# MLP: the 64-row products of fc1 in pairs, six tiles of a pass held open together

## The chip, the cores and the metric

One core of a Trainium2 chip (trn2) runs the whole program. The metric is the device time of one execution in microseconds (us), as the median of several runs. Engines are named as in the profile: PE is TensorE (PEld its weight loads), DVE is VectorE, ACT is ScalarE, POOL is GpSimd, SP is the engine that issues the DMAs.

## The reference

One transformer block with modulation on x of 2 x 2048 tokens by 576 channels. Only its last part matters here:

```
C = 576; FF = 2304
h = modulate(layernorm(x), shift_mlp, scale_mlp)
mlp = gelu(h @ W_fc1 + b_fc1, approximate=True) @ W_fc2 + b_fc2
x = x + gate_mlp * mlp
```

The contraction of fc1 has 576 terms: four blocks of 128 and a last one of 64.

## The kernel before

The program runs in phases, one after the other; attention takes the largest part, and `phase_mlp` is the last. Tokens go in 8 chunks of 512 (`CH`, `NCH = 8`), hidden channels in two halves of 1152 (`FF // 2`). A pass n (0 to 15, `NN`) takes one chunk through one half: passes 0 to 7 the first half, 8 to 15 the second; `ORDER` sets which chunk.

**fc1 of a pass** makes 9 tiles (`NT`; f = 0 to 8) of 128 hidden channels by 512 tokens, each in one PSUM bank. Every float32 operand is split into a high and a low part of type fp32r. For each of the four blocks of 128 rows there are three products (high x high, high x low of the tokens, low of the weights x high). The last block has 64 rows only. `wm` holds its high weights twice, in rows 0 to 63 and again in 64 to 127; `hh[..][:, 4, :]` holds the tokens' high part in rows 0 to 63 and their low part in 64 to 127, so that one product gives both terms. `wr` holds the low weights in rows 0 to 63 and zeros in 64 to 127 (a memset on POOL, awaited through `s_z`); product 14 of a tile multiplies it by the same 128 rows. So a tile is 14 products of 128 rows (`passes`, L42 on), a pass 126.

**fc2 of a pass** makes 8 tiles (4 groups of 128 tokens by 2 halves of 288 channels), each from 27 products (9 f by 3), in the four banks `pm`. fc1 uses the four banks `pf` in turn (pass 0 also `pm`).

The order on each engine is written out by hand, and semaphores tie them. Per f: PE ends tile f and raises `s_f1`; ACT applies gelu (L2110) into `af[m % 2]`, after the low part of tile f-2 is done (`s_al`); DVE writes the high part `ah` (CAST, L2060) and the low part `al` (TENSOR_TENSOR, L2062). The first tile of fc2 waits for `s_al` of f ahead of its products with f. Two further jobs are hung on the same f loop of ACT and DVE:

- in passes whose successor's tokens are still whole in DRAM (n + 1 in `WHOLE`, that is n = 1 to 6 and 9 to 14), ACT splits one block of the next pass's tokens after the gelu of f = 2 to 6 (`high_h`, L2099), DVE makes its low part (`low_h`, L2045 and L2048);
- in pass 8, after each f one piece of W_fc2's second half: `high` on ACT (L2090), `low` on DVE (L2038). fc2 of pass 8 waits for piece f too ahead of its first products with f.

DVE ends each fc2 tile with two operations (L2075, L2081). POOL adds a bias to a block of y (L2129) once it has landed. PE's sequence in a pass is 126 products of fc1, then 216 of fc2.

Of the kernel before, what the change touches and what calls it, by code (L numbers as in the profile page):

```python
# [7 lines left out]
F = mybir.dt.float32  # L8
# [230 lines left out]
class Ahead:  # L239
# [4 lines left out]
    def __init__(self, S, hh, hl, b1, new, kf):  # L244
        self.hh, self.hl, self.b1 = hh, hl, b1
        self.oi = S.sb("oi", [128, KT, CH])
        stg = self.oi[:, :, :].rearrange("p k t -> p (k t)")
        self.stg = [stg[:, i * C:(i + 1) * C] for i in range(4)]
        self.pf = [S.ps(f"pf{i}", [128, 512]) for i in range(4)]
        G = FF // 6  # L250
        self.wide = [stg[:, i * G:(i + 1) * G] for i in range(6)] + [kf[:, i * G:(i + 1) * G] for i in range(4)]
        self.wh, self.wl, self.wm, self.wr = new
        self.s_w, self.s_f1, self.s_b1, self.s_hs = S.sems("w", 4), S.sem("f1"), S.sem("b1"), S.sem("hs")
        self.s_whi, self.s_wlo, self.s_z = S.sem("whi"), S.sem("wlo"), S.sem("z")

    def load(self, e, j, W):

# [8 lines left out]
    def split(self, j):  # L266

        g, kt = divmod(j, KT)
        cols = slice(g * FF // 6, (g + 1) * FF // 6)
        return (self.wh[:, kt, cols], self.wl[:, kt, cols]) if kt < 4 else (self.wm[:, cols], self.wr[0:64, cols])  # L270


class FirstThird:
# [26 lines left out]
    def low(self, e, kt, stg):  # L300
        w = stg[kt % 2]
        e.wait_ge(self.hi, kt + 1)
        if kt < 4:
            e.tensor_tensor(self.wl[:, kt, :], w[:, self.n], self.wh[:, kt, :].bitcast(F), ALU.subtract).then_inc(
                self.lo, 1)
        else:
            e.tensor_tensor(self.wr[0:64, :], w[0:64, self.n], self.wm[0:64, :].bitcast(F), ALU.subtract).then_inc(
                self.lo, 1)


def program(nc, x, cond, W_qkv, b_qkv, W_proj, b_proj, W_fc1, b_fc1, W_fc2, b_fc2, W_ada, b_ada, out):
# [1094 lines left out]
def phase_proj(nc, A, W, rest, first, N, ident, ks0, adaT, eps, gd, xf, ot, sm, W_fc1, b_fc1, hth, htl, hw,  # L1406
# [366 lines left out]
    def gpsimd(e):  # L1773
        rest.add(e)
        for kind, c, n in work():
# [26 lines left out]
            elif kind == "weights":  # L1802
                if n == 0:
# [5 lines left out]
                    e.wait_ge(N.s_z, 1)  # L1809
                hi, lo = N.split(n)  # L1810
                rows = slice(0, 128 if n < 4 else 64)
                e.wait_ge(N.s_whi, n + 1)
                e.tensor_tensor(lo, N.wide[n][rows], hi[rows].bitcast(F), ALU.subtract).then_inc(N.s_wlo, 1)

    with nc.Block() as block:
        block.sync(sync)
# [6 lines left out]
def phase_mlp(nc, A, first, N, gd, hth, htl, hw, y1, y2, of, W_fc1, b_fc1, W_fc2, b_fc2):  # L1823
# [38 lines left out]
    def piece(k):  # L1862

        half, j = divmod(k, 24)
        if j < 15:
            g, kt = divmod(j, 5)
            cs, c0 = slice((g - 1) * G3, g * G3), half * FH + g * G3
            if g == 0:
                to = (first.wh[:, kt, :], first.wl[:, kt, :]) if kt < 4 else (first.wm, first.wr[0:64, :])
            else:  # L1870
                to = (wh[:, kt, cs], wl[:, kt, cs]) if kt < 4 else (wm[:, cs], wr[0:64, cs])
            return (W_fc1, kt * 128, 128 if kt < 4 else 64, c0, G3) + to
        j -= 15
        return W_fc2, half * FH + j * 128, 128, 0, C, vh[:, j, :], vl[:, j, :]
# [46 lines left out]
    def sync(e):  # L1921
# [11 lines left out]
        def load(n):  # L1933
# [44 lines left out]
        for i in range(4):  # L1978
            e.wait_ge(s_w[i], total[i])
        for i in range(2):  # L1980
            e.wait_ge(s_h[i], 32)
            e.wait_ge(s_yi[i], 32 * NN)
            e.wait_ge(s_yo[i], 32 * NN)
        e.wait_ge(N.s_hs, 64)
# [1 line left out]
        e.wait_ge(s_c, 64)  # L1986

    def tensor(e):
        for n in range(NN):
            i, half = n % 2, n // NCH  # L1990
            if n in WHOLE:
                e.wait_ge(s_hlo, KT * WHOLE.index(n) + KT)
            elif n > 1:
                e.wait_ge(s_h[i], 32)
            for f in range(4 if n == 0 else 0, NT):
                m = NT * n + f
                if n in (0, NCH) and f % 3 == 0:
                    e.wait_ge(s_whi, W1[half] + 5 * (f // 3 + 1) - DONE)
                    e.wait_ge(s_wlo, W1[half] + 5 * (f // 3 + 1) - DONE)
                if m > 7:  # L2000
                    e.wait_ge(s_af, m - 3)
                if f < 3:
                    pairs = passes(first.wh, first.wl, first.wm, first.wr, hh[i], hl[i],
                                   slice(f * 128, f * 128 + 128), slice(0, CH))
                else:
                    pairs = passes(wh, wl, wm, wr, hh[i], hl[i], slice((f - 3) * 128, (f - 3) * 128 + 128),
                                   slice(0, CH))
                for p, (w, a) in enumerate(pairs):
                    ins = e.matmul(tile(m)[:, :], w, a, start=p == 0, stop=p == 13)  # L2009
                ins.then_inc(s_f1, 1)  # L2010
            for t in range(4):
                ts = slice(t * 128, t * 128 + 128)
                for n2 in range(2):
                    m = 8 * n + 2 * t + n2
                    cs = slice(n2 * HALF, (n2 + 1) * HALF)
                    if m > 3:
                        e.wait_ge(s_ug, m - 3)
                    else:
                        e.wait_ge(s_af, m + 5)
# [65 lines left out]
    def scalar(e):  # L2085
# [6 lines left out]
        def high_h(n, kt):  # L2092

            e.wait_ge(s_hw, 48 * (WHOLE.index(n) + 1))
            if kt == 0:
                e.wait_ge(s_f1, NT * (n - 1))
                if n == 3:
                    e.wait_ge(N.s_hs, 64)
            e.activation(hh[n % 2][:, kt, :], hw_in[:, kt, :], ACT.Copy).then_inc(s_hhi, 1)  # L2099

        for n in range(NN):
            half = n // NCH
            for f in range(NT):
# [53 lines left out]
```

## Time and profile before

| | us |
|---|---|
| median of 3 runs | 3420.9 (3420.76 to 3423.96) |
| profiled execution | 3421.19 |
| its span, first to last instruction | 3419.5 |
| PE busy | 3403.6 (100% of the span) |
| DVE busy | 1982.8 (58%) |
| ACT busy | 1488.7 (44%) |

The profiled execution stands 0.3 us over the median; 1.7 us of it lie outside the span. A row of the timeline begins with its start in us from the span's start and its duration in us; durations of neighbours on one engine overlap, since each holds the time through the pipeline, so the pace is read from starts.

### The profile page before, as it was taken

What the parts mean: (1) busy time and instruction counts of PE and PEld (TensorE: products, weight loads), DVE (VectorE), ACT (ScalarE), POOL (GpSimd) and SP (SyncE); (2) the same over time, 40 slices, a digit from 0 to 9 for tenths busy, and PEclk for the clock granted to TensorE, in tenths of its full rate; (3) what the DMA queues carried; (4) which work ended last, traced back from release to release, by engine and by line L of the source; (5) the groups of instructions that cost most, each with busy time, mean ns of one, the idle gap of its engine ahead of it and who ended that gap; (6) DMA issues with size and microseconds to landing.
All of it is one profiled execution on the core that took longest, in us unless ns stands there. A gap on an engine that the chain in (4) does not pass through costs nothing. (4 is left out here: it accounts for less than half of the span.)

```text
span 3419.5 us, 46642 instructions
## 1 busy us (share of the span) xinstructions
PE 3403.6 (100%) x17036; PEld 2281.4 (67%) x17036; DVE 1982.8 (58%) x3592; ACT 1488.7 (44%) x2793; POOL 361.6 (11%) x284
## 2 busy tenths in 40 slices
PE   9999999999999999999999999999999999999999
PEld 7888854544545545545545545447989999898988
DVE  6446576776776766776766766754653333433332
ACT  3322365555555555555555555565531111211110
POOL 0000010111100000010000000015610101000000
PEclk9999999999999999999999999999999999999999
DMA  7553421212112121111211111115751212321211
GB/s 229 177 185 108 155 78 30 65 41 61 38 34 51 31 55 30 47 40 33 55 31 51 34 36 49 31 39 163 262 165 51 80 51 95 121 83 44 77 53 53
DMA packets 131908, 265.89 MB, mean 78 GB/s; under 512 B 17427, under 2 KB 38675, under 8 KB 124770
## 3 DMA queue, kind: packets, MB, share of 16 engines
q1 hardware_dynamic: 131686, 262.91, 25.5%
q8 instruction: 142, 2.33, 0.3%
q14 instruction: 80, 0.66, 0.1%
HBM read 164.50 MB, written 97.26 MB: 77 GB/s over the span
## 5 line engine op out<-in xcount | busy, mean ns | idle before, releaser
L1259 DVE TENSOR_REDUCE q_mx<-b_sp 128x1 f32<-128x512 f32 x1968 | 1196.3, 677 | 228.1 <-PE b_sp L1197 228.1
L1316 ACT ACTIVATE b_pt<-b_st 128x512 f32<-128x512 f32 x2009 | 1013.4, 626 | 441.2 <-PE b_st L1214 434.0
L1227 PE MATMUL b_op<-b_pt,b_vs 128*37 128x512 f32 x4096 | 929.4, 596 | 0.0
L1227 PEld LDWEIGHTS b_op<-b_pt,b_vs 128*37 128x37 f32 x4096 | 223.6, 113 | 567.3 <-issue 440.3
L2110 ACT ACTIVATE d_af<-n_pf,q_mx 128x512 f32<-128x512 f32 x140 | 96.3, 688 | 702.0 <-PE n_pf L2009 701.5
L2027 PE MATMUL d_pm<-d_vh,d_ah 128*128 128x288 f32 x1152 | 339.3, 295 | 0.5 <-DVE d_al L2062 0.5
L2028 PE MATMUL d_pm<-d_vl,d_ah 128*128 128x288 f32 x1152 | 339.4, 295 | 0.0
L2029 PE MATMUL d_pm<-d_vh,d_al 128*128 128x288 f32 x1152 | 339.3, 295 | 0.0
L1382 POOL TENSOR_TENSOR w_oc<-b_oa,b_ob 37x512 f32<-37x512 f32 x127 | 163.0, 1283 | 1588.4 <-DVE b_ob L1292 1582.3
L1197 PE MATMUL b_sp<-q_hh,q_lo 108*128 108x512 f32 x688 | 284.2, 413 | 0.9 <-PEq L1001 0.9
L1214 PE MATMUL b_st<-q_qs,q_ks 110*128 110x512 f32 x697 | 275.4, 396 | 0.0
L1214 PE MATMUL b_st<-q_lo,q_hh 110*128 110x512 f32 x672 | 264.0, 397 | 0.0
L1197 PE MATMUL b_sp<-q_ks,q_qs 108*128 108x512 f32 x640 | 263.7, 412 | 0.0
L1197 PE MATMUL b_sp<-b_ks,b_qs 108*128 108x512 f32 x640 | 263.6, 412 | 0.0
L1292 DVE COPY b_ob<-b_op 37x512 f32<-37x512 f32 x127 | 86.7, 683 | 292.3 <-PE b_op L1227 292.3
L1214 PE MATMUL b_st<-b_qs,b_ks 110*128 110x512 f32 x640 | 253.3, 396 | 0.0
L1324 ACT ACTIVATE b_oa<-b_op 37x512 f32<-37x512 f32 x127 | 75.6, 595 | 347.8 <-PE b_op L1227 347.8
L2027 PEld LDWEIGHTS d_pm<-d_vh,d_ah 128*128 128x128 f32 x1152 | 216.2, 188 | 1.4 <-issue 0.7
L2028 PEld LDWEIGHTS d_pm<-d_vl,d_ah 128*128 128x128 f32 x1152 | 216.1, 188 | 0.7
L2029 PEld LDWEIGHTS d_pm<-d_vh,d_al 128*128 128x128 f32 x1152 | 216.2, 188 | 0.0
L2075 DVE TENSOR_TENSOR d_ug<-d_pm,d_gt 128x288 f32<-128x288 f32 x128 | 58.5, 457 | 250.8 <-PE d_pm L2029 250.7
L2060 DVE CAST d_ah<-d_af 128x512 fp32r<-128x512 f32 x144 | 63.3, 440 | 240.9 <-ACT d_af L2110 240.9
(366 smaller groups left out, 4755.0 us busy)
## 6 DMA issues: line engine op xcount, KB each, us to landing
qkh<-a_th SPq DMA_DIRECT2D x72, 256.0 KB, 2.0
qkl<-a_tl SPq DMA_DIRECT2D x72, 256.0 KB, 2.1
d_yi<-y SPq DMA_DIRECT2D x64, 288.0 KB, 3.0
n_oi<-hw SPq DMA_DIRECT2D x12, 1024.0 KB, 5.9
vd<-a_vx SPq DMA_DIRECT2D x8, 1184.0 KB, 6.3
b_vs<-vd SPq DMA_DIRECT2D x32, 296.0 KB, 2.8
a_x<-in_x SPq DMA_DIRECT2D x8, 1152.0 KB, 6.3
ot<-w_oc SPq DMA_DIRECT2D x128, 72.0 KB
```

What stands on the lines that cost most here:

```text
L1197: e.matmul(sp[slot % 4][:, :], qs[i][0:108, qb * 128:qb * 128 + 128], ks[i][0:108, k4 * 512:k4 * 512 + 512], start=True, stop=True).then_i ...
L1214: e.matmul(bank(x)[:, :], ks[i][0:110, kb * 128:kb * 128 + 128], qs[i][0:110, u * 512:u * 512 + 512], start=True, stop=True).then_inc(s_st, 1)
L1227: ins = e.matmul(op[64 * a:64 * a + VW, :], vs[h % 2][:, 2 * j + a, :], pt[g % NP][:, a * 512:a * 512 + 512], start=j == 0, stop=j == 7)
L1259: e.tensor_reduce(mx[:, k // 4, k % 4:k % 4 + 1], sp[slot % 4][:, :], AX.X, ALU.max).then_inc(s_mx, 1)
L1292: e.tensor_copy(ob[i][:, :], op[0:VW, :]).then_inc(s_oa, 1)
L1316: e.activation(pt[g % NP][:, a * 512:a * 512 + 512], bank(x)[:, :], ACT.Exp, scale=SCALE).then_inc(s_p, 1)
L1324: e.activation(oa[i][:, :], op[64:64 + VW, :], ACT.Copy).then_inc(s_oa, 1)
L1382: e.tensor_tensor(oc[i][:, :], oa[i][:, :], ob[i][:, :], ALU.add).then_inc(s_oc, 1)
L2027: e.matmul(out, ah[:, f, ts], vh[:, f, cs], start=f == 0, stop=False)
L2028: e.matmul(out, ah[:, f, ts], vl[:, f, cs], start=False, stop=False)
L2029: ins = e.matmul(out, al[:, f, ts], vh[:, f, cs], start=False, stop=f == NT - 1)
L2110: e.activation(af[m % 2][:, :], tile(m)[:, :], ACT.Gelu_apprx_tanh, bias=b1[:, half * NT + f:half * NT + f + 1]).then_inc(s_af, 1)
```

## The change

fc1 uses a ring of eight banks (`pf` and `pm`). In passes 1 to 15 tiles 0 to 5 (`GROUP = 6`) run 13 products each and stay open. After tile 5's 13th the six last products follow in a row (`last_products`): those of even f use rows 0 to 63 of `wr` and `hh`, those of odd f rows 64 to 127 of `wr` and of a new tensor `hx`, a copy of the tokens' high part of the last block in rows 64 to 127. `wr` now holds the low weights in both halves; memset and `s_z` are gone. Tiles 6 to 8 have 14 products as before, and so has pass 0. `hx` lies in parts of old tensors and is written by an additional ACT copy ahead of the split of block 4, or by an additional DMA for passes 1, 8 and 9.

```diff
         g, kt = divmod(j, KT)
-        return (self.wh[:, kt, cols], self.wl[:, kt, cols]) if kt < 4 else (self.wm[:, cols], self.wr[0:64, cols])
+        return (self.wh[:, kt, cols], self.wl[:, kt, cols]) if kt < 4 else (self.wm[:, cols], self.wr[:, cols])
...
+        self.hx = [w[64:128, :, FF // 6:FF // 6 + 128] for w in (w0.wl, w0.wh)]
...
-                    e.memset(N.wr[64:128, :].bitcast(F), 0.0).then_inc(N.s_z, 1)
-                    e.wait_ge(N.s_z, 1)
...
-    def tile(m):
-        return pm[m - 4] if 4 <= m < 8 else pf[m % 4]
+    def bank(n, f):
+        ring = pf + pm if n == 0 else pf[0:1] + pm + pf[1:4]
+        return ring[f % 8]
+    GROUP = 6
...
+            e.dma_start(hx[i].bitcast(F), hth[4, 0:64, rows].rearrange("p (k t) -> p k t", k=4)).then_inc(s_h[i], 16)
+        e.dma_start(hx[1].bitcast(F), hh[1][0:64, 4, :].bitcast(F).rearrange("p (k t) -> p k t", k=4)).then_inc(s_h[1], 16)
...
+        def bank_free(n, f):
+            if f >= 8:
+                e.wait_ge(s_af, NT * n + f - 8 + 1)
+            elif n and 1 <= f < 5:
+                e.wait_ge(s_ug, 8 * (n - 1) + 4 + f)
+            elif n:
+                e.wait_ge(s_af, NT * n)
+        def last_products(n):
+            i = n % 2
+            if n == 1:
+                e.wait_ge(s_h[i], 16)
+            for f in range(GROUP):
+                w, c0 = (first.wr, f * 128) if f < 3 else (wr, (f - 3) * 128)
+                if f % 2 == 0:
+                    e.matmul(bank(n, f)[:, :], w[0:64, c0:c0 + 128], hh[i][0:64, 4, :], start=False,
+                             stop=True).then_inc(s_f1, 1)
+                else:
+                    e.matmul(bank(n, f)[:, :], w[64:128, c0:c0 + 128], hx[i], start=False, stop=True).then_inc(s_f1, 1)
...
-                if m > 7:
-                    e.wait_ge(s_af, m - 3)
+                bank_free(n, f)
...
-                for p, (w, a) in enumerate(pairs):
+                for p, (w, a) in enumerate(pairs[0:13] if grouped else pairs):
...
+                if grouped and f == GROUP - 1:
+                    last_products(n)
...
+            if kt == 4:
+                e.activation(hx[n % 2], hw_in[64:128, kt, :].rearrange("p (k t) -> p k t", k=4), ACT.Copy)
             e.activation(hh[n % 2][:, kt, :], hw_in[:, kt, :], ACT.Copy).then_inc(s_hhi, 1)
```

PE before, pass 2, where tile 0 ends and tile 1 begins (`q_hh0` is `hh[0]`, `e_wr0` the first third of `wr`):

```order
L2009 MATMUL n_pf2<-q_hh0,e_wl0 128x512
L2009 MATMUL n_pf2<-q_hh0,e_wm0 128x512
L2009 MATMUL n_pf2<-q_hh0,e_wr0 128x512
L2009 MATMUL n_pf3<-q_hh0,e_wh0 128x512 [waits d_s_af]
L2009 MATMUL n_pf3<-q_lo0,e_wh0 128x512
```

PE of the changed kernel, pass 2, where tile 5's 13th product ends and tile 6 begins (`e_wl0` stands for `hx[0]`, `z_wr` for the rest of `wr`):

```order
L2034 MATMUL n_pf1<-q_hh0,z_wl 128x512
L2034 MATMUL n_pf1<-q_hh0,z_wm 128x512
L2010 MATMUL n_pf0<-q_hh0,e_wr0 128x512
L2013 MATMUL d_pm0<-e_wl0,e_wr0 128x512
L2010 MATMUL d_pm1<-q_hh0,e_wr0 128x512
L2013 MATMUL d_pm2<-e_wl0,z_wr 128x512
L2010 MATMUL d_pm3<-q_hh0,z_wr 128x512
L2013 MATMUL n_pf1<-e_wl0,z_wr 128x512
L2034 MATMUL n_pf2<-q_hh0,z_wh 128x512 [waits d_s_af]
```

The last product of tile 0, which stood ahead of tile 1, now stands behind tile 5's 13th, and with it `s_f1` of tiles 0 to 4 comes later.

ACT before, around the split of block 4 for the next pass (`n_oi` holds the landed tokens):

```order
L2099 ACTIVATE q_hh0<-n_oi 128x512 [waits d_s_hw]
L2110 ACTIVATE d_af1<-n_pf3,q_mx 128x512 [waits d_s_al,n_s_f1]
L2099 ACTIVATE q_hh0<-n_oi 128x512 [waits d_s_hw]
L2110 ACTIVATE d_af0<-n_pf0,q_mx 128x512 [waits d_s_al,n_s_f1]
```

The same place of the changed kernel:

```order
L2129 ACTIVATE q_hh0<-n_oi 128x512 [waits d_s_hw]
L2140 ACTIVATE d_af1<-n_pf2,q_mx 128x512 [waits d_s_al,n_s_f1]
L2128 ACTIVATE e_wl0<-n_oi 64x4x128 [waits d_s_hw]
L2129 ACTIVATE q_hh0<-n_oi 128x512
L2140 ACTIVATE d_af0<-n_pf3,q_mx 128x512 [waits d_s_al,n_s_f1]
```

One copy is added; the order of the rest, and all of DVE's order in the f loop, is the same.

## Rows read from the trace of the kernel before

**Rows 1.** The page, part 1: busy time and share of each engine.

```profile
PE 3403.6 (100%) x17036; PEld 2281.4 (67%) x17036; DVE 1982.8 (58%) x3592; ACT 1488.7 (44%) x2793; POOL 361.6 (11%) x284
```

**Rows 2.** PE's waits, 2480 us to the end: waiter, releaser, us, times, longest.

```profile
PE d_pm L2027 <- DVE d_al L2062: 0.5, 1, 0.5
PE d_pm L2009 <- PEq L1815: 0.3, 1, 0.3
```

**Rows 3.** Timeline, PE: fc1 and fc2 of pass 4, first product of pass 5.

```profile
2721.60 0.40 PE L2009 MATMUL n_pf<-q_hh,e_wh 128*128 128x512 f32 x1
...
2750.60 0.40 PE L2009 MATMUL n_pf<-q_hh,z_wr 128*128 128x512 f32 x1
2750.84 0.30 PE L2027 MATMUL d_pm<-d_vh,d_ah 128*128 128x288 f32 x1
2750.97 0.30 PE L2028 MATMUL d_pm<-d_vl,d_ah 128*128 128x288 f32 x1
...
2779.48 0.39 PE L2009 MATMUL n_pf<-e_ah,e_wh 128*128 128x512 f32 x1
```

**Rows 4.** Timeline, PE, attention: out of and into products in column halves (L1227).

```profile
1499.78 1.89 PE L1227 MATMUL b_op<-b_pt,b_vs 128*37 128x512 f32 x8
1501.60 0.50 PE L1197 MATMUL b_sp<-q_hh,q_lo 108*128 108x512 f32 x1
1501.93 0.39 PE L1214 MATMUL b_st<-b_qs,b_ks 110*128 110x512 f32 x1
...
1505.24 0.39 PE L1214 MATMUL b_st<-b_qs,b_ks 110*128 110x512 f32 x1
1505.56 0.63 PE L1227 MATMUL b_op<-b_pt,b_vs 128*37 128x512 f32 x2
```

**Rows 5.** Timeline, PEld then PE, near 55 us: products of 64 rows (L668).

```profile
54.87 0.09 PEld L668 LDWEIGHTS a_sp<-a_wa,g_sc 128*2 128x2 f32 x2 [0.15 <-issue]
55.45 0.09 PEld L668 LDWEIGHTS a_sp<-a_wa,g_sc 64*2 64x2 f32 x4 [0.49 <-issue]
...
54.87 0.66 PE L668 MATMUL a_sp<-a_wa,g_sc 128*2 128x288 f32 x4
...
55.69 0.41 PE L668 MATMUL a_sp<-a_wa,g_sc 64*2 64x288 f32 x2
56.03 0.50 PE L705 MATMUL a_pm<-q_hh,a_wh 128*128 128x512 f32 x1
56.37 0.39 PE L705 MATMUL a_pm<-q_lo,a_wh 128*128 128x512 f32 x1
56.60 0.40 PE L705 MATMUL a_pm<-q_hh,a_wl 128*128 128x512 f32 x1
```

**Rows 6.** Timeline, DVE, pass 4: tiles 2 and 3, and tile 6.

```profile
2732.16 1.33 DVE L2060 CAST d_ah<-d_af 128x512 fp32r<-128x512 f32 x1 [2.05 <-ACT d_af L2110]
2733.53 0.69 DVE L2062 TENSOR_TENSOR d_al<-d_af,d_ah 128x512 fp32r<-128x512 f32 x1
2734.14 0.69 DVE L2045 TENSOR_TENSOR q_qs<-n_oi,e_ah 128x512 fp32r<-128x512 f32 x1
...
2745.69 0.69 DVE L2062 TENSOR_TENSOR d_al<-d_af,d_ah 128x512 fp32r<-128x512 f32 x1
2746.41 0.69 DVE L2048 TENSOR_TENSOR e_ah<-n_oi,e_ah 64x512 fp32r<-64x512 f32 x1
```

**Rows 7.** Timeline, DVE, pass 0, behind its work: no idle time between rows.

```profile
2512.45 0.42 DVE L2060 CAST d_ah<-d_af 128x512 fp32r<-128x512 f32 x1
2512.90 0.69 DVE L2062 TENSOR_TENSOR d_al<-d_af,d_ah 128x512 fp32r<-128x512 f32 x1
2513.51 0.42 DVE L2060 CAST d_ah<-d_af 128x512 fp32r<-128x512 f32 x1
```

**Rows 8.** Timeline, DVE, pass 8: two tiles in a row without idle time.

```profile
2968.64 0.42 DVE L2060 CAST d_ah<-d_af 128x512 fp32r<-128x512 f32 x1
2969.10 0.69 DVE L2062 TENSOR_TENSOR d_al<-d_af,d_ah 128x512 fp32r<-128x512 f32 x1
2969.71 0.75 DVE L2038 TENSOR_TENSOR d_vl<-n_oi,d_vh 128x576 fp32r<-128x576 f32 x1
2970.38 0.42 DVE L2060 CAST d_ah<-d_af 128x512 fp32r<-128x512 f32 x1
```

**Rows 9.** Timeline, ACT, pass 4: gelu and split.

```profile
2725.03 0.69 ACT L2110 ACTIVATE d_af<-n_pf,q_mx 128x512 f32<-128x512 f32 x1 [31.16 <-PE n_pf L2009]
...
2731.44 0.69 ACT L2110 ACTIVATE d_af<-n_pf,q_mx 128x512 f32<-128x512 f32 x1 [2.52 <-PE n_pf L2009]
2732.03 0.62 ACT L2099 ACTIVATE e_ah<-n_oi 128x512 fp32r<-128x512 f32 x1
```

**Rows 10.** Timeline, POOL: the memset ahead of `phase_mlp`, and pass 4.

```profile
2486.16 0.73 POOL L1808 MEMSET z_wr<- 64x768 f32 x1 [11.69 <-PE n_pf L1651]
...
2731.78 1.43 POOL L2129 TENSOR_TENSOR d_yi<-d_yi,d_gb 128x576 f32<-128x576 f32 x1 [11.39 <-DMA d_yi<-y]
```

**Rows 11.** DMA issues: KB each, median us from issue to landing.

```profile
n_oi<-in_L_cond_W_fc SPq DMA_DIRECT2D x18, 288.0 KB, 4.4
```

More of the change, by code:

```diff
@@ L253, in __init__ @@
         self.s_w, self.s_f1, self.s_b1, self.s_hs = S.sems("w", 4), S.sem("f1"), S.sem("b1"), S.sem("hs")
-        self.s_whi, self.s_wlo, self.s_z = S.sem("whi"), S.sem("wlo"), S.sem("z")
+        self.s_whi, self.s_wlo = S.sem("whi"), S.sem("wlo")
     def load(self, e, j, W):
@@ L306, in low @@
         else:
-            e.tensor_tensor(self.wr[0:64, :], w[0:64, self.n], self.wm[0:64, :].bitcast(F), ALU.subtract).then_inc(
-                self.lo, 1)
+            e.tensor_tensor(self.wr, w[:, self.n], self.wm.bitcast(F), ALU.subtract).then_inc(self.lo, 1)
 def program(nc, x, cond, W_qkv, b_qkv, W_proj, b_proj, W_fc1, b_fc1, W_fc2, b_fc2, W_ada, b_ada, out):
@@ L1807, in gpsimd @@
                     e.wait_ge(first.lo, KT)
-                    e.memset(N.wr[64:128, :].bitcast(F), 0.0).then_inc(N.s_z, 1)
-                    e.wait_ge(N.s_z, 1)
                 hi, lo = N.split(n)
-                rows = slice(0, 128 if n < 4 else 64)
                 e.wait_ge(N.s_whi, n + 1)
-                e.tensor_tensor(lo, N.wide[n][rows], hi[rows].bitcast(F), ALU.subtract).then_inc(N.s_wlo, 1)
+                e.tensor_tensor(lo, N.wide[n], hi.bitcast(F), ALU.subtract).then_inc(N.s_wlo, 1)
     with nc.Block() as block:
@@ L1838, in phase_mlp @@
     hh, hl = N.hh, N.hl
+    hx = first.hx
     af = [A.sb(f"af{i}", [128, CH]) for i in range(2)]
@@ L1868, in piece @@
             if g == 0:
-                to = (first.wh[:, kt, :], first.wl[:, kt, :]) if kt < 4 else (first.wm, first.wr[0:64, :])
+                to = (first.wh[:, kt, :], first.wl[:, kt, :]) if kt < 4 else (first.wm, first.wr)
             else:
-                to = (wh[:, kt, cs], wl[:, kt, cs]) if kt < 4 else (wm[:, cs], wr[0:64, cs])
+                to = (wh[:, kt, cs], wl[:, kt, cs]) if kt < 4 else (wm[:, cs], wr[:, cs])
             return (W_fc1, kt * 128, 128 if kt < 4 else 64, c0, G3) + to
@@ L1980, in sync @@
         for i in range(2):
-            e.wait_ge(s_h[i], 32)
+            e.wait_ge(s_h[i], (48, 64)[i])
             e.wait_ge(s_yi[i], 32 * NN)
@@ L1993, in tensor @@
             elif n > 1:
-                e.wait_ge(s_h[i], 32)
+                e.wait_ge(s_h[i], (48, 64)[i])
             for f in range(4 if n == 0 else 0, NT):
-                m = NT * n + f
+                grouped = n and f < GROUP
                 if n in (0, NCH) and f % 3 == 0:
@@ L2007, in tensor @@
                                    slice(0, CH))
-                for p, (w, a) in enumerate(pairs):
-                    ins = e.matmul(tile(m)[:, :], w, a, start=p == 0, stop=p == 13)
-                ins.then_inc(s_f1, 1)
+                for p, (w, a) in enumerate(pairs[0:13] if grouped else pairs):
+                    ins = e.matmul(bank(n, f)[:, :], w, a, start=p == 0, stop=p == 13)
+                if not grouped:
+                    ins.then_inc(s_f1, 1)
+                if grouped and f == GROUP - 1:
+                    last_products(n)
             for t in range(4):
@@ L2015, in tensor @@
                     cs = slice(n2 * HALF, (n2 + 1) * HALF)
-                    if m > 3:
+                    if m % 8 < 4:
+                        e.wait_ge(s_af, NT * n + m % 4 + (5 if n == 0 else 2))
+                    else:
                         e.wait_ge(s_ug, m - 3)
-                    else:
-                        e.wait_ge(s_af, m + 5)
                     for f in range(NT):
@@ L2033, in low @@
         def low(k):
-            src, _, rows, _, cols, hi, lo = piece(k)
+            cols, hi, lo = piece(k)[4:7]
             there(e, k)
@@ L2037, in low @@
             old_read(e, k)
-            e.tensor_tensor(lo, staged(k)[0:rows, 0:cols], hi[0:rows].bitcast(F), ALU.subtract).then_inc(s_wlo, 1)
+            e.tensor_tensor(lo, staged(k)[:, 0:cols], hi.bitcast(F), ALU.subtract).then_inc(s_wlo, 1)
         def low_h(n, kt):
@@ L2109, in scalar @@
                     e.wait_ge(s_al, m - 1)
-                e.activation(af[m % 2][:, :], tile(m)[:, :], ACT.Gelu_apprx_tanh,
+                e.activation(af[m % 2][:, :], bank(n, f)[:, :], ACT.Gelu_apprx_tanh,
                              bias=b1[:, half * NT + f:half * NT + f + 1]).then_inc(s_af, 1)
```

## The prediction

> **What bounds the kernel now.** First the page's busy times: PE is busy for 3403.6 of 3419.5 us, DVE for 58% and ACT for 44% [rows 1]. Then PE's waits in the last 940 us, which hold `phase_mlp`: two, of 0.5 and 0.3 us, both in pass 0 [rows 2]. So passes 1 to 15 are an unbroken stream of products, and only two things can change the time: how long PE's own stream is, and a wait that does not exist today. The granted clock is 1.00 throughout, the upper of its two levels (2.4 GHz), and I expect it to stay.
>
> Next the pace of that stream, from starts on PE's timeline [rows 3]. fc1 of pass 4 has 126 products; the first starts at 2721.60, the last at 2750.60: 29.00 / 125 = 0.232 us each. fc2 has 216 from 2750.84 to the next pass at 2779.48: 28.64 / 216 = 0.1326 each.
>
> **Part 1: PE's stream.** Removed per pass: six products of 128 rows, 6 x 0.232 = 1.39 us. Added: three pairs of 64 rows. Nothing in the trace shows two products side by side in the two halves of the rows. Nearest are the products in the two halves of the columns: eight of them take four steps, (1.89 - 0.59) / 3 = 0.43 us per pair, and one alone would need that much, since these are plain float32 products in two runs [rows 4]. So pairs do overlap there, and I take 0.232 us for a pair. Bounds: 0.43 / 2 = 0.215 below; 0.464 (no overlap at all) above.
>
> The array is then used in another division, and the trace has a price for going there and back. Out of the column halves: the last pair starts at 1499.78 + 1.89 - 0.59 = 1501.08, the next product at 1501.60, that is 0.52 for a pair of 0.43, so 0.09 more; the product after that starts 0.33 later and not 0.23, so 0.10 more, and its neighbour's record is 0.50 long for 0.39: its weight load is not hidden [rows 4]. Into them: 1505.24 to 1505.56 is 0.32 for 0.23, again 0.09 more [rows 4]; the weights there have 37 columns only, here 128, so I take the 0.10 for the load too. Does it also hold for rows? Going from 128 to 64 rows near 55 us, a pair that starts near 55.12 is followed at 55.45, and that one by the next at 55.69: 0.33 against 0.24; going back, 55.69 to 56.03 to 56.37 is 0.34 and 0.34 against 0.24 and 0.23 [rows 5]. The same 0.09 to 0.10 and 0.10. So the group costs 3 x 0.232 + 2 x (0.09 + 0.10) + 0.01 for the second product of a pair = 1.09 us (1.087), and a pass gains 1.39 - 1.09 = 0.30 us. Fifteen passes: **4.5 us gained**, of 10.4 that halving the six products alone would give.
>
> Two rules of the Trainium skill would make this less. TensorE: Matmul & The Clock Gate (Part 3, Measured speedup) reports 3.07 times for four row tiles, not 4; as an estimate from that share a pair would take 0.30 us, and the gain fall by 3.2 us in all. The same page (Part 3, the per-tile semaphore tail) puts 26 ns on each further increment of a semaphore in a group; six products here raise `s_f1`, an estimated 2 us over 15 passes if PE had to wait for them. No run so far shows either; the sum leaves both out.
>
> **Part 2: what waits for the group.** `s_f1` of tiles 0 to 5 now comes almost at once, some 18 us into fc1, and ACT and DVE have tiles 6 to 8 and the start of fc2 to do what they did during the whole of fc1. ACT's steps are shorter than DVE's (gelu to split starts 0.59 apart [rows 9]; the added copy for `hx`, some 0.6, stands once between tiles 6 and 7), and gelu of f needs only `al` of f-2, so DVE sets the pace. Its costs without idle time: CAST to TENSOR_TENSOR 0.45, on to the next CAST 0.61, a tile 1.06 [rows 7]; with a split of 512 columns another 0.61, a tile 1.68 [rows 6, 7]; tile 6 with the split of the half block 0.72 in place of 0.61 [rows 6], 1.79.
>
> Let E be the start of the first pair. Tile 0 ends at E + 0.50, gelu starts 0.02 later (in pass 4 tile 0 ends near 2725.01, gelu starts at 2725.03 [rows 3, 9]), and the CAST 0.72 after gelu's start (2731.44 to 2732.16 [rows 6, 9]): E + 1.24. The CAST of tile 8 starts 1.06 x 2 + 1.68 x 4 + 1.79 + 1.06 = 11.69 later, and `al` of 8 is ready after 0.45 + 0.69 + 0.03 more: **E + 14.10**. PE needs it at: the pairs and the way back, E + 0.89; tiles 6 to 8, 0.10 + 42 x 0.232 = 9.84, so fc2 starts at E + 10.73; 24 products later, 3.18, it wants f = 8: **E + 13.91**. So PE waits 0.19 us, in the 12 passes with splits: **2.3 us lost**. In passes 7 and 15 DVE has nothing else and keeps up with PE: tile 8 ends 0.16 into fc2, `al` is ready 0.02 + 0.72 + 0.45 + 0.69 + 0.03 later, at 2.07, 1.1 ahead of the 3.18. In pass 1 to 6 today one CAST takes 1.33 instead of 0.43 while POOL works [rows 6, 10]; that falls 10 us into the pass, where DVE now has no tile, so it costs nothing.
>
> In **pass 8** each tile has a piece of W_fc2: 2968.64 to 2970.38, 1.74 a tile [rows 8]. Piece 8 is ready at E + 1.24 + 8 x 1.74 + 0.46 + 0.61 + 0.75 + 0.03 = E + 17.01, wanted at E + 13.91: **3.1 us lost**. Piece f+4 is requested when piece f is done, lands 4.4 us later [rows 11], and is used 4 x 1.74 = 7 after the request, its ACT copy of 0.7 included: about 1 us to spare.
>
> **Part 3: the rest.** The wider low parts run over more partitions at the same columns, so at the same time; the memset on POOL ended near 2486.9 [rows 10] and PE never waited for it [rows 2]. The additional DMAs for `hx` stand in SP's queue ahead of the weight pieces of passes 0 and 8, half a microsecond each: in pass 8 the pieces are wanted 18 us later than now, so it is hidden; in pass 0 the first pieces are wanted early, where PE already waits 0.5 us [rows 2], at most 0.5 more. Banks: tile 8 waits for gelu of tile 0, started 6 us before; tiles 1 to 4 wait for the last fc2 tiles of the pass before, at least one tile of 3 us ahead. Nothing to pay.
>
> **Sum.** 3421.19 - 4.5 + 2.3 + 3.1 = 3422.1 for the profiled execution, which is 0.3 above the median of its kernel: **3421.8 us**, 0.9 over today's median. About 0.2% (6.8 us) is what a measurement of this kernel can tell from no change.
>
> **Rivals.**
> - *No overlap of the pairs.* Six products in a row at 0.232 plus the two changes of division: 6 x 0.232 + 0.38 = 1.77 for 1.39, +0.38 a pass, +5.7 us; DVE then has 0.7 us more per pass, so the 2.3 vanish and 3.1 become 2.4: +8.1, **3429.0**, slower. For it: no row shows row halves side by side. Against it: the column halves do overlap [rows 4]. It decides once a pair takes more than about 0.42 us. 12%.
> - *DVE's lateness is larger.* The 0.19 is a small difference of two long sums, and each 1% on DVE's 13 us is 0.13 us in 12 passes, 1.6 us. If DVE's tiles were 5% longer while packed (say 1.76 with a split): +0.6 a pass, +7.8, with pass 8: **3430**. Against it: the packed rows of passes 0 and 8 are measured at that density [rows 7, 8]. 4%.
> - *DVE is in time.* The same small difference the other way: -2.3 from the sum, and pass 8 somewhat cheaper: **3419**. 16%.
> - *No change of division is paid, or loads stay hidden.* The 0.38 a pass goes, -5.7; but all is then earlier for PE, DVE's lateness grows by about 0.28 in each of the 13 passes, +3.7: **3420**. 6%. Only with DVE in time as well does it pass 6.8 us: -10.4 + 3: **3413**, 3%.
>
> The rest, 59%, is the forecast. Added up by their times: **within 0.2% 0.81, slower 0.16, faster 0.03**. The range goes from 3417.0 (DVE in time, pair at 0.215, pass 8 cheaper) to 3428.0 (the second load of a first pair not hidden either, 15 x 0.10 = 1.5; DVE 0.3 later in 13 passes, 3.9), which leaves out the two slower rivals and the 3% below.
>
> **What the new profile would show.** Part 1: on PE's timeline pairs that start 0.01 apart and 0.23 from each other, 0.32 ahead of the first, and 0.32 and 0.33 behind the last; single starts 0.23 apart mean the first rival. Part 2: a wait of the first fc2 product of f = 8 (L2055 there) for `al`, near 0.2 us in 12 passes, none in passes 7 and 15, and near 3 us in total for the split pieces or `al` in pass 8; DVE without idle time from tile 0 to tile 8. What would make it wrong: another price for the changes of division, or DVE or ACT slower packed than in rows 6 to 9.

## The result and the profile after

| | before | changed |
|---|---|---|
| median of 19 runs, us | 3421.86 (3420.11 to 3424.77) | 3428.60 (3426.21 to 3431.03) |
| ratio, 95% interval | | 1.0020 (1.0014 to 1.0027) |
| profiled execution, us | 3421.19 | 3428.88 |
| its span, us | 3419.5 | 3427.1 |

The change made the kernel 6.7 us slower, 0.2%. I had forecast 3421.8 and no change, with a range that ended at 3428.0: the measured time lies above it.

The page's first lines and PE's waits from 2480 us on (columns as in [rows 2]), against [rows 1] and [rows 2]:

```profile
PE 3407.1 (99%) x17036; PEld 2273.6 (66%) x17036; DVE 1968.3 (57%) x3592; ACT 1492.1 (44%) x2805; POOL 360.7 (11%) x283
```

```profile
PE d_pm L2055 <- DVE d_al L2090: 2.7, 8, 1.1
PE d_pm L2055 <- DVE d_vl L2066: 2.2, 2, 1.1
PE d_pm L2034 <- PEq L1812: 0.3, 1, 0.3
PE d_pm L2055 <- issue: 0.2, 1, 0.2
```

PE, which waited 0.5 us for DVE before, now waits 4.9. The list counts only idle time between records; short waits hide under the pipeline of the product ahead, so starts tell more. From the starts on PE's timeline, the length of each part of a pass (us; odd and even passes apart where they differ; the differences are summed before rounding):

| | before | changed | difference in all |
|---|---|---|---|
| start of `phase_mlp`'s first product | 2502.4 | 2503.6 | +1.2 |
| pass 0, fc2 | 29.36 | 30.66 | +1.3 |
| fc1, 8 odd passes | 29.15 | 28.87 | -2.2 |
| fc1, 7 even passes | 29.24 | 28.94 | -2.1 |
| fc2, passes 1, 3, 5, 9, 11, 13 | 28.63 | 29.09 | +2.7 |
| fc2, passes 2, 4, 6, 10, 12, 14 | 28.64 | 29.00 | +2.1 |
| fc2, pass 7 (and 15) | 28.64 | 28.63 | 0 |
| fc2, pass 8 | 28.64 | 33.31 | +4.7 |

The sum is 7.7, and that is all of the difference of the two spans (7.6 as rounded above). So the pairs gave what they were to give, 4.4 us, and fc2 lost 4.9 in the 12 passes with splits, 4.7 in pass 8 and 1.3 in pass 0; 1.2 more lie ahead of the phase.

**The pairs**, PE's timeline of pass 4, against [rows 4] and [rows 5]:

```profile
2742.31 0.39 PE L2034 MATMUL n_pf<-q_hh,z_wm 128*128 128x512 f32 x1
2742.63 0.50 PE L2010 MATMUL n_pf<-q_hh,e_wr 64*128 64x512 f32 x1
2742.64 0.50 PE L2013 MATMUL d_pm<-e_wl,e_wr 64*128 64x512 f32 x1
2742.98 0.39 PE L2010 MATMUL d_pm<-q_hh,e_wr 64*128 64x512 f32 x1
2742.98 0.39 PE L2013 MATMUL d_pm<-e_wl,z_wr 64*128 64x512 f32 x1
2743.20 0.39 PE L2010 MATMUL d_pm<-q_hh,z_wr 64*128 64x512 f32 x1
2743.21 0.39 PE L2013 MATMUL n_pf<-e_wl,z_wr 64*128 64x512 f32 x1
2743.53 0.50 PE L2034 MATMUL n_pf<-q_hh,z_wh 128*128 128x512 f32 x1
2743.87 0.39 PE L2034 MATMUL n_pf<-q_lo,z_wh 128*128 128x512 f32 x1
```

The two products of a pair start 0.01 apart or together; the second pair starts 0.34 behind the first, the third 0.22 behind the second. Going into the half rows costs 0.32 from start to start where 0.23 is the pace, and going out 0.32 again; behind each of the two the next step is 0.34, with the 0.50 record of a weight load that is not hidden. From 2742.31 to 2743.87 is 1.56, where eight steps of 0.232 took 1.86: 0.30 gained.

**DVE behind the group**, its first and last tiles and tile 6 in pass 4, against [rows 6] and [rows 7]; then PE at f = 8 of fc2:

```profile
2743.89 0.43 DVE L2088 CAST d_ah<-d_af 128x512 fp32r<-128x512 f32 x1 [18.24 <-ACT d_af L2140]
2744.35 0.69 DVE L2090 TENSOR_TENSOR d_al<-d_af,d_ah 128x512 fp32r<-128x512 f32 x1
...
2752.68 0.42 DVE L2088 CAST d_ah<-d_af 128x512 fp32r<-128x512 f32 x1
2753.14 0.69 DVE L2090 TENSOR_TENSOR d_al<-d_af,d_ah 128x512 fp32r<-128x512 f32 x1
2753.86 0.69 DVE L2076 TENSOR_TENSOR e_ah<-n_oi,e_ah 64x512 fp32r<-64x512 f32 x1
2754.58 0.43 DVE L2088 CAST d_ah<-d_af 128x512 fp32r<-128x512 f32 x1
...
2755.65 0.42 DVE L2088 CAST d_ah<-d_af 128x512 fp32r<-128x512 f32 x1
2756.11 0.69 DVE L2090 TENSOR_TENSOR d_al<-d_af,d_ah 128x512 fp32r<-128x512 f32 x1
```

```profile
2756.46 0.29 PE L2057 MATMUL d_pm<-d_vh,d_al 128*128 128x288 f32 x1
2756.86 0.40 PE L2055 MATMUL d_pm<-d_vh,d_ah 128*128 128x288 f32 x1
2757.09 0.29 PE L2056 MATMUL d_pm<-d_vl,d_ah 128*128 128x288 f32 x1
```

(`al` is the TENSOR_TENSOR behind each CAST.) DVE stood idle for 18.24 us, then worked without a break from 2743.89 to the end of `al` of tile 8 near 2756.80, and PE's product with f = 8 starts 0.40 behind its neighbour where 0.13 is the pace: 0.27 of wait. The next start is 0.23 later and not 0.13: its weight load (0.40 record) was not hidden. That second part, 0.10, belongs to the wait.

**Pass 8**, PE's timeline at f = 6, 7 and 8 of fc2:

```profile
2987.56 0.37 PE L2055 MATMUL d_pm<-d_vh,d_ah 128*128 128x288 f32 x1 [0.24 <-issue]
...
2989.29 0.37 PE L2055 MATMUL d_pm<-d_vh,d_ah 128*128 128x288 f32 x1 [1.10 <-DVE d_vl L2066]
...
2991.02 0.57 PE L2055 MATMUL d_pm<-d_vh,d_ah 128*128 128x288 f32 x1 [1.10 <-DVE d_vl L2066]
2991.39 0.44 PE L2056 MATMUL d_pm<-d_vl,d_ah 128*128 128x288 f32 x1
2991.63 0.44 PE L2057 MATMUL d_pm<-d_vh,d_al 128*128 128x288 f32 x1
2991.87 0.44 PE L2055 MATMUL d_pm<-d_vh,d_ah 128*128 128x288 f32 x1
```

PE waits for three pieces in turn (0.4, 1.3 and 1.3 us beyond the pace of 0.13), and then twelve products start 0.24 apart and not 0.13. The stage table gives the reason; its columns are the stretch and its length, the busy time (and instructions) of PE, PEld, DVE, ACT and POOL, the granted clock, the DMA share and GB/s:

```profile
2984.80:2990.00 5.20, 3.77 (x25) 3.14 (x23) 5.10 (x10) 2.52 (x4) 0.00 (x0) 1.00 0.37 113
2990.00:2993.00 3.00, 1.98 (x8) 2.01 (x9) 1.77 (x4) 0.00 (x0) 0.00 (x0) 0.67 0.00 0
```

The granted clock fell from 1.00 to a mean of 0.67 in the 3 us, with starts at the pace of 1.2 GHz: 288 columns in 0.24 us. In the stretch ahead PE was busy for 3.77 of 5.20 us. I had expected the clock to stay.

DVE has no idle time in this pass either, from tile 0 to the last piece:

```profile
2975.24 0.43 DVE L2088 CAST d_ah<-d_af 128x512 fp32r<-128x512 f32 x1 [16.59 <-ACT d_af L2140]
...
2990.17 0.75 DVE L2066 TENSOR_TENSOR d_vl<-n_oi,d_vh 128x576 fp32r<-128x576 f32 x1
```

So PE waited for DVE's sum, and DVE for no load.

### The profile page after: what moved, and what is told of

It reads as the page before. It is cut to its first block and busy times, and to the rows that moved or that the text cites. A ratio compares the mean times of both kernels' runs of the same rounds, so it can differ in the third digit from the quotient of the medians.

```text
span 3427.1 us, 46655 instructions
## 1 busy us (share of the span) xinstructions
PE 3407.1 (99%) x17036; PEld 2273.6 (66%) x17036; DVE 1968.3 (57%) x3592; ACT 1492.1 (44%) x2805; POOL 360.7 (11%) x283
## 5 line engine op out<-in xcount | busy, mean ns | idle before, releaser
L2140 ACT ACTIVATE d_af<-n_pf,q_mx 128x512 f32<-128x512 f32 x80 | 54.7, 685 | 699.6 <-PE d_pm L2013 671.3
L1198 PEld LDWEIGHTS b_sp<-q_hh,q_lo 108*128 108x128 f32 x688 | 130.1, 189 | 103.3 <-issue 76.4
```

What stands on the lines that cost most here:

```text
L1198: e.matmul(sp[slot % 4][:, :], qs[i][0:108, qb * 128:qb * 128 + 128], ks[i][0:108, k4 * 512:k4 * 512 + 512], start=True, stop=True).then_i ...
```

## Experiments

All from the changed kernel. fc2 lengths are from PE's starts in the profiled execution. Medians under one heading come from one chip and are set against the kernel before on that chip. All keep the whole computation. In six of these kernels (`ungrouped`, `full_rows`, `split_first`, `hx_late`, `group4`, `after_again`) the profiled execution was the fastest of eleven or within 0.1 us of it, and the median lies 1.2 to 3.4 us over it: that part is in no trace, and the causes below are read from the lengths of the parts.

### Which part costs: four kernels on one chip (before: 3421.29)

**ungrouped**: every tile keeps its 14 products.

```diff
-                grouped = n and f < GROUP
+                grouped = False
```

> The changed kernel with the group undone: every tile has its 14 products of 128 rows one after another; the ring of eight banks, the wider wr and the copies into hx stay. My theory (the loss lies in ACT's and DVE's work being packed behind the group, and in pass 0 in the DMA for hx that stands ahead of the weight pieces): passes 1 to 15 as before (fc1 29.15 and 29.24 us, fc2 28.63), pass 0 some 1.3 us longer, so 1.3 us over the kernel before. Rival (the ring of banks or the copies cost something themselves): a wait or a longer fc1 or fc2 in passes 1 to 15, up to all of the 4 to 5 us lost in fc2 there.

Passes 1 to 15 are as before to 0.01 us in both parts; fc2 of pass 0 takes 30.29. Ring, wider low parts and copies cost nothing in the passes; the rival falls. Median 3424.10, ratio 1.0007 (0.9998 to 1.0016): 2.8 over the kernel before, of which pass 0 explains 0.9. I had expected 1.3; the rest is taken up below.

**full_rows**: the six last products stay together, with 128 rows each.

```diff
-                if f % 2 == 0:
-                    e.matmul(bank(n, f)[:, :], w[0:64, c0:c0 + 128], hh[i][0:64, 4, :], start=False,
-                             stop=True).then_inc(s_f1, 1)
-                else:
-                    e.matmul(bank(n, f)[:, :], w[64:128, c0:c0 + 128], hx[i], start=False, stop=True).then_inc(s_f1, 1)
+                e.matmul(bank(n, f)[:, :], w[:, c0:c0 + 128], hh[i][:, 4, :], start=False, stop=True).then_inc(s_f1, 1)
```

> The changed kernel with the six last products kept together behind tile 5, but each with all 128 rows, so no pair and no change of the array's division. PE has 0.3 us a pass more than the changed kernel. My theory (DVE's chain behind the group against PE's tiles 6 to 8): tile 0 ends 0.39 after the start E' of the first of the six, al of tile 8 is ready at E' + 14.1, and is wanted at E' + 6 x 0.232 + 9.74 + 3.18 = E' + 14.3: no wait in the 12 passes with splits, in pass 8 a wait of some 2.5 us plus what restarts cost; 1.3 us in pass 0. Sum 4.5 to 5.5 us over the kernel before. Rival (the change of division itself disturbs what follows, and fc2's waits come from there): the waits near f = 8 of fc2 go, and pass 8 loses little as well.

fc1 29.17 and 29.25, fc2 28.63 in the 12 passes, no wait; pass 8 31.30 (+2.7), pass 0 30.28. Median 3427.45, ratio 1.0017 (1.0008 to 1.0025), 6.2 over the kernel before where I expected 4.5 to 5.5. PE's waits for DVE (the first line is pass 8, the second pass 0):

```profile
PE d_pm L2051 <- DVE d_vl L2062: 2.2, 2, 1.1
PE d_pm L2051 <- DVE d_al L2086: 1.1, 1, 1.1
```

So pass 8 loses by the gathering alone, with no change of the array's division; the rival falls. And the 12 passes sit on an edge: with 0.3 us more of PE's work, and DVE's first CAST 1.15 instead of 1.26 us behind the group's start, their wait is gone.

**split_first**: the split of the next pass's tokens ahead of the f loop, on ACT and DVE alike.

```diff
+            for kt in range(KT if n + 1 in WHOLE else 0):
+                low_h(n + 1, kt)
             for f in range(NT):
...
-                if 2 <= f < 2 + KT and n + 1 in WHOLE:
-                    low_h(n + 1, f - 2)
```

> The changed kernel with the split of the next pass's tokens (ACT and DVE, five blocks) moved ahead of the gelu of tile 0, where both engines wait for PE. My theory: DVE's chain behind the group is 5 x 0.61 us shorter, al of tile 8 is ready 1.1 us ahead of its use, and the waits in fc2 (0.37 and 0.45 us a pass with the restart) go in all 12 passes: 4.9 us under the changed kernel; pass 8 and pass 0 stay as they are. Rival (ACT or semaphores set the lateness, not DVE's sum): less than half of it.

fc2 28.63 and 28.62 in all 12 passes, fc1 unchanged at 28.87 and 28.94, pass 8 33.31. The waits of the 12 passes are gone to the last, 4.9 us as expected. Span 3419.4; median 3422.33, ratio 1.0005 (0.9996 to 1.0014). The experiment moves work of ACT too, but in the changed kernel ACT had idle time behind the group and waited for DVE, as here before the gelu of tile 8 of pass 4:

```profile
2753.93 0.69 ACT L2140 ACTIVATE d_af<-n_pf,q_mx 128x512 f32<-128x512 f32 x1 [0.77 <-DVE d_al L2090]
```

So DVE's sum behind the group was the cause. In pass 8 the clock fell here as well:

```profile
2980.00:3016.00 36.00, 33.53 (x228) 32.37 (x227) 12.93 (x26) 2.44 (x4) 0.00 (x0) 0.95 0.24 75
```

The mean clock of this whole execution is listed as 1.00 all the same: one such stretch is too short to show in it.

**hx_late**: the first DMA into `hx` behind the loads of W_fc2.

```diff
-        e.dma_start(hx[1].bitcast(F), hh[1][0:64, 4, :].bitcast(F).rearrange("p (k t) -> p k t", k=4)).then_inc(s_h[1], 16)
         for k in range(W2[0], W2[0] + 4):
             load_w(k)
...
+        e.dma_start(hx[1].bitcast(F), hh[1][0:64, 4, :].bitcast(F).rearrange("p (k t) -> p k t", k=4)).then_inc(s_h[1], 16)
         rows = slice(CH, 2 * CH)
```

> The changed kernel with the first DMA into hx moved from the head of SP's queue to behind the loads of W_fc2 in pass 0. My theory (the load of the pieces is late because of it): the 1.3 us by which fc2 of pass 0 grew go, 1.3 us under the changed kernel. Rival (pass 0 varies by itself from run to run): pass 0 stays long.

fc2 of pass 0 29.18, 1.5 less than in the changed kernel's profile; median 3425.97, ratio 1.0012 (1.0003 to 1.0021). SP's timeline of pass 0, changed kernel:

```profile
2503.52 0.69 SPq L1954 DMA_DIRECT2D e_wh<-e_ah  x1
2504.26 2.04 SPq L1934 DMA_DIRECT2D n_oi<-in_L_cond_W_fc  x4
...
2509.61 8.70 SPq L1934 DMA_DIRECT2D n_oi<-in_L_cond_W_fc  x5
```

The same in this kernel:

```profile
2501.98 1.76 SPq L1934 DMA_DIRECT2D n_oi<-in_L_cond_W_fc  x4
...
2508.07 7.25 SPq L1934 DMA_DIRECT2D n_oi<-in_L_cond_W_fc  x5
```

The fifth piece is issued 6.05 us behind the phase's first product in both (2503.56 and 2502.02), so the 0.7 at the head did not delay that issue. What came later is the landing. ACT's split of the fifth and sixth pieces, the waits for all nine loads, and their times from issue to landing, in the changed kernel:

```profile
2516.41 1.41 ACT L2118 ACTIVATE d_vh<-n_oi 128x576 fp32r<-128x576 f32 x2 [1.89 <-DMA n_oi<-in_L_cond_W_fc]
  ACT d_vh L2118: 3.3, 4
DMA to landing us min/median/max: 3.1/5.2/6.8
```

The same in this kernel:

```profile
2512.86 1.34 ACT L2118 ACTIVATE d_vh<-n_oi 128x576 fp32r<-128x576 f32 x2
  ACT d_vh L2118: 0.5, 1
DMA to landing us min/median/max: 2.6/3.8/4.8
```

Counted from the phase's start, that split begins at 12.85 and at 10.84. The ninth piece needs the buffer of the fifth, so its issue, the last of the five, is late too: that is the 8.70 for 7.25, and the 1.5 of fc2. Why the loads land so much later behind a DMA that was issued in 0.69 us is not shown.

This kernel's pass 8 also shows the clock's part: the same three waits, but 31.79 and not 33.31. Its stage table has 1.00 for all of fc2 of pass 8, the changed kernel's 0.95:

```profile
2981.80:3013.60 31.80, 29.33 (x217) 28.69 (x216) 12.50 (x25) 2.53 (x4) 0.00 (x0) 1.00 0.24 75
```

```profile
2984.79:3018.10 33.31, 30.86 (x218) 30.26 (x216) 12.44 (x25) 2.52 (x4) 0.00 (x0) 0.95 0.23 72
```

So the waits of pass 8 are 3.15 us, and 1.5 is the fall of the clock behind them. Not every execution has it. With the same three waits the profiles of the changed kernel (33.31), `split_first` (33.31) and `after_again` (33.08) have 10 to 13 starts 0.24 apart, that of `hx_late` (31.79) none. With two waits, `one_half` (1.1 and 1.3 us; 32.60) has them and `full_rows` (1.3 and 1.3; 31.30) does not. What decides is not shown.

### The overlap, the size of the group, and a better version (before: 3421.16)

**one_half**: both kinds of last product in rows 0 to 63.

```diff
-                    e.matmul(bank(n, f)[:, :], w[64:128, c0:c0 + 128], hx[i], start=False, stop=True).then_inc(s_f1, 1)
+                    e.matmul(bank(n, f)[:, :], w[0:64, c0:c0 + 128], hh[i][0:64, 4, :], start=False,
+                             stop=True).then_inc(s_f1, 1)
```

> The changed kernel with the last products of odd tiles also in rows 0 to 63 (the same weights and tokens as in rows 64 to 127), so that no two lie in different halves. My theory (the gain is the overlap of the halves): starts 0.23 apart, fc1 6 x 0.232 + 0.39 instead of 3 x 0.232 + 0.39, 29.56 and 29.63 us; DVE is then in time in the 12 passes, pass 8 loses 2.5 and not 3.2. Rival (64 rows are cheaper by themselves): fc1 stays near 28.9.

```profile
2741.94 0.50 PE L2010 MATMUL n_pf<-q_hh,e_wr 64*128 64x512 f32 x1
2742.28 0.39 PE L2013 MATMUL d_pm<-q_hh,e_wr 64*128 64x512 f32 x1
2742.51 0.39 PE L2010 MATMUL d_pm<-q_hh,e_wr 64*128 64x512 f32 x1
2742.75 0.39 PE L2013 MATMUL d_pm<-q_hh,z_wr 64*128 64x512 f32 x1
```

On PE's timeline single starts 0.23 apart: a product of 64 rows is no cheaper than one of 128. fc1 29.59 and 29.64, fc2 28.63 in the 12 passes, 32.60 in pass 8 (its clock fell too). Median of five 3432.39, ratio 1.0031 (1.0018 to 1.0044): my first rival as it would have been, 11.2 us over the kernel before and not 8.1, since pass 0 and the clock cost here too.

**group4**: `GROUP = 4`.

```diff
-    GROUP = 6
+    GROUP = 4
```

> The changed kernel with four tiles in the group and not six. The two changes of division cost the same 0.39 us, the two pairs save only 2 x 0.232: fc1 0.07 us shorter than before (29.08 and 29.16). ACT and DVE have tiles 4 to 8 (16 us) to catch up: no wait in fc2 in any pass, pass 8 among them. With some 1 us more in pass 0 the sum is that of the kernel before, within 0.5 us. Rival (any gathering of last products costs in fc2): waits near f = 8 as with six.

fc1 29.11 and 29.17, fc2 28.63 in every pass but 0 (30.55), and no waits but there. Median 3422.25, ratio 1.0004 (0.9995 to 1.0013), 1.1 over the kernel before and not within 0.5; its span is 3418.4. Four tiles cost nothing in fc2, and gain next to nothing, since the change of division costs 0.38 whatever the group holds.

**pieces_first**: four pieces of W_fc2 split ahead of tile 0 in pass 8, five behind tiles 0 to 4.

```diff
+    AHEAD = 4
+    def split_at(n, f):
+        if n != NCH:
+            return pieces(n, f=f)
+        k = W2[1] + AHEAD + f
+        return range(k, min(k + 1, W2[1] + NT))
+    def split_ahead(n):
+        return range(W2[1], W2[1] + AHEAD) if n == NCH else range(0)
...
+            for k in split_ahead(n):
+                low(k)
...
-                for k in pieces(n, f=f):
+                for k in split_at(n, f):
                     low(k)
```

ACT's loop has the same with `high(k)`.

> The changed kernel with the first four pieces of W_fc2's second half split ahead of the gelu of tile 0 in pass 8, and the other five behind tiles 0 to 4. My theory (in pass 8 DVE's sum of nine pieces behind the group is what fc2 waits for): four pieces of 0.67 us leave the chain, al of tile 8 is ready at E + 14.3 for a use at E + 14.0, so fc2 of pass 8 takes 29.1 us and not 31.8 to 33.3; 2.7 us under the changed kernel, 4.2 where its clock had also fallen to 1.2 GHz behind the waits. The 12 passes with splits and pass 0 stay as they are. Rival (the loads of the pieces, not DVE, set the end of pass 8): it stays over 31 us.

fc2 of pass 8 29.18; the rest as in the changed kernel. Median 3423.99, ratio 1.0007 (0.9998 to 1.0016). The rival (over 31) falls. Splitting four pieces early also requests later loads sooner, so this alone does not part DVE's sum from the loads; that DVE had no idle time in pass 8 of the changed kernel does.

**all_early**: `split_first`, `pieces_first` and `hx_late` together; their diffs are above.

> The changed kernel with three moves at once: the split of the next pass's tokens and four pieces of pass 8 ahead of the gelu of tile 0, the first DMA into hx behind the loads of pass 0. My theory: only the gain of the pairs is left, 15 x 0.29 = 4.4 us, against 0.4 in pass 8: 3.9 us under the kernel before, fc1 28.87 and 28.94, fc2 28.63, pass 0 as before. Rival (work moved ahead collides with what stood there, as POOL's operation and the loads): waits elsewhere, and the time stays at that of the kernel before.

fc1 28.87 and 28.94, fc2 28.63 and 28.62, pass 0 29.35, pass 8 29.18. PE's waits from 2520 us on:

```profile
PE d_pm L2068 <- DVE d_al L2107: 0.8, 2, 0.5
```

Median 3416.89, ratio **0.9988 (0.9979 to 0.9997)**: 4.3 under the kernel before.

### Again, changed and moved kernel on one chip (before: 3421.38)

> The changed kernel as it is, to stand beside the next run on the same chip: 6 to 7 us over the kernel before. Passes as in its first profile: fc1 28.87 and 28.94, fc2 29.1 and 29.0 in the 12 passes with splits, pass 0 30.6; pass 8 31.8, or 33.3 where the clock falls to 1.2 GHz behind its waits (both were seen in the profiles of kernels with the same pass 8).

3428.59, 7.2 over the kernel before, ratio 1.0020 (1.0011 to 1.0029); pass 0 30.55, pass 8 33.08, the rest as in the first profile.

> The kernel with the splits, four pieces and the DMA for hx moved, a second time. My theory: again some 4 us under the kernel before, and 10 to 11 us under the changed kernel on the same chip: 4.9 from the 12 passes, 2.7 to 4.2 from pass 8, 1.3 from pass 0, the rest from restarts at the lower clock. Rival (its gain was chance of one chip): within 1 us of the kernel before.

3417.57, ratio 0.9987 (0.9978 to 0.9996), 11.0 under the changed kernel. The rival falls: the gain is there a second time.

### What was left of pass 0 (before: 3420.89)

> The changed kernel without the group, a second time, beside the next run on one chip. Its profile had only 0.9 us more in pass 0, its median 2.8 us, and 7 of its 11 executions a mean clock of 0.999. My theory (the DMA for hx at the head of SP's queue makes pass 0 wait, and behind such waits the clock falls to 1.2 GHz in a part of the executions): again 2 to 3 us over the kernel before, with half or more of the executions at 0.999.

3421.92, ratio 1.0004 (0.9995 to 1.0013), fc2 of pass 0 30.72. But none of its 11 executions had a mean clock of 0.999. What my theory foretold (falls of the clock brought on by the DMA, 2 to 3 us) did not come: 1.0 us is what comes again. It is not refuted for single executions, since one fall does not show in a mean of 1.00.

> The same with the DMA for hx behind the loads of pass 0. My theory: pass 0 as before (29.2 to 29.4 us), the time within 0.5 us of the kernel before, and 0.999 as rare as there (2 of 33). Rival (the copies into hx on ACT, the wider low parts or the missing memset in the phase ahead cause the falls of the clock): the time stays 2 us over the kernel before, 0.999 stays frequent.

(`ungrouped` and `hx_late` together.) 3420.82, ratio 1.0001 (0.9992 to 1.0010), pass 0 29.21, 1.00 in all 11. Without group and early DMA no cost of the change is left.

Open stays why 7 of 11 executions of `ungrouped` showed 0.999 the first time, where the kernel before had it in 2 of 33. Those seven took 3425.2 us on average, the other four 3421.4, so the 2.8 us lie in them; but only the profiled execution has a trace, and that one was at 1.00.

## Why the prediction was wrong

From 0.9 us forecast to 7.7 measured between the two profiles, 6.8 are missing: 2.6 in the waits of the 12 passes, 1.5 from a fall of the clock in pass 8, 1.3 in pass 0, 1.2 ahead of the phase, 0.1 in the pairs, and rounding. Three terms of the prediction failed: the wait in the 12 passes was mis-sized, and the clock and pass 0 stood at nothing or next to it.

**Part 1 was right.** Changes of division taken from the column halves [rows 4] and from 64 rows [rows 5] held to 0.01 us, the pairs overlap, and the gain was 4.4 for 4.5. A pair takes 0.22 to 0.23 us, and the product behind the six raises of `s_f1` starts 0.32 after the last pair, which the change of division alone explains. By the two rules of the Trainium skill (TensorE: Matmul & The Clock Gate, Part 3) that the prediction weighs, it would have been an estimated 0.30 a pair and a tail behind the group; neither shows in PE's starts. The prediction gave no row for its word that one plain float32 product alone would need 0.43 us, on which the overlap of the column halves rests. The trace of before has one:

```profile
2464.40 0.60 PE L1615 MATMUL c_pt<-g_ident,c_xn 128*128 128x128 f32 x4
```

Four single ones of 128 columns, 0.27 each by their record, are (0.60 - 0.27) / 3 = 0.11 apart, so 512 columns are 0.44. That such a product is made in two runs no row shows; only the doubled time does.

**Part 2 had the right mechanism and the wrong size**, and this is the step that failed most. For the 12 passes I had 2.3, measured 4.9:

- *The wait itself*: 0.27 in even passes and 0.34 in odd ones for 0.19. With E = 2742.63, `al` of tile 8 releases PE at E + 14.23 (I had 14.10), and PE wants it at E + 13.96 (13.91). Most of it is one instruction: the split of the half block delays not only its own start, by 0.72 for 0.61, but also the next CAST, 0.72 again (2753.86 to 2754.58), in all 12 passes alike. [rows 6] show the first gap; behind this split DVE was idle in the kernel before, so the second could not be read. In pass 5, odd, PE is there at E + 13.87. About 1.4 us over 12 passes.
- *The restart*: behind each wait the next start is 0.10 late in even passes and 0.11 in odd ones, since the weight load is no longer hidden. I had priced this very 0.10 twice for the changes of division [rows 4], and left it out for a wait: 6 x 0.10 + 6 x 0.11 = 1.3 us.

I called the 0.19 a small difference of two long sums and gave only 4% to the case that it is larger. Both omissions could only make it larger, and the trace of before had no pass in which DVE works nine tiles with splits in a row, against which to check the sum. The upper end of the range was not its own sum either: 3421.8 + 1.5 + 3.9 is 3427.2, and it stood at 3428.0.

**Pass 8**: 3.1 predicted; without a fall of the clock it was 3.15. The 1.5 on top I had excluded by "I expect it to stay", though my own sum had PE idle for 3.1 of the first 6.3 us of fc2 (E + 10.73 to E + 17.01). That waits of this density are followed by a fall in some executions could not be read from the trace of before, which has no such stretch in `phase_mlp`.

**Part 3, pass 0**: nothing, at most 0.5; measured 1.3, and 1.5 less when undone. I priced the DMA by its issue (half a microsecond; 0.69 measured). The pieces behind it landed up to 2 us later, the last of them is requested only when the fifth is split, and PE already waited for the end of this chain.

**What is no part of the change**: 1.2 us ahead of `phase_mlp`. About 2462 us both executions wait for ACT; in the changed one twelve starts behind it are 0.24 apart. The stage tables of 2460 to 2465, before and then changed, give 1.00 and 0.70:

```profile
2460.00:2465.00 5.00, 2.95 (x24) 2.96 (x25) 4.96 (x12) 4.04 (x9) 4.08 (x5) 1.00 0.36 99
```

```profile
2460.00:2465.00 5.00, 3.32 (x15) 3.33 (x16) 4.96 (x13) 3.71 (x8) 4.11 (x5) 0.70 0.41 123
```

The second profiled execution of the changed kernel starts its phase at 2501.0, sooner than the kernel before (2502.4), so this comes and goes, and nothing shows it as a loss of the change.

**The rivals**: no overlap (12%) fell by the pairs' starts; DVE in time (16%) fell by the waits; free changes of division (6%) fell. DVE's lateness larger (4%) is the one that came: 0.22 more a pass than the forecast 0.19, restart included, where it had set 0.6 more. It came by one gap and the restart, and not by DVE's tiles being 5% longer.

## What to carry to other kernels

When work of one engine is gathered, write down what every engine behind it does in that loop, including jobs that only hang there for convenience; move those into the idle time that the gathering itself creates before judging the gain. A wait in a packed stream costs its length plus one unhidden weight load (0.10 us here), and, if several come in a row, in some executions the lower clock as well. A DMA put at the head of a chain of loads can cost more than its issue, here 1.5 us for 0.69: look at when the loads behind it land.

## What the runs showed of the hardware

- Two products of 64 rows in different halves of the array's rows, writing different banks, start 0.01 us apart and take 0.22 to 0.23 us together for 512 columns of fp32r; one alone takes 0.23, as one of 128 rows does.
- Going from 128 rows to 64 and back costs 0.09 + 0.10 us each way; leaving the column halves costs the same, and entering them 0.09 and 0.03 (the weights there have 37 columns).
- The split on 64 partitions, which writes over one of its inputs, starts 0.72 behind the operation ahead, and the next one 0.72 behind it, where one on 128 partitions with an output of its own had 0.61. Which of the two differences does it is not shown.
- Three waits within 4 us, 0.4, 1.3 and 1.3 long, were followed by 10 to 13 starts at the pace of 1.2 GHz in three profiled executions and by none in a fourth, with the same kernel code in that pass.
